# Last attention of a four-part block: head sums kept with heads on partitions, sorted by DMA, divided on GpSimd

## The chip, the cores and the metric

One core of one Trainium2 chip runs the whole program. The metric is the device time of one execution in microseconds (us); the median of the runs stands for the kernel.

## What is computed

The reference is a block of four residual parts on x of shape (4, 1024, 256): a cross attention, an expert layer, a second cross attention with 16 heads, and a last self attention with 16 heads of 16 channels over 4096 tokens in 4 batches. The change concerns the last part alone:

```
qkv = x @ W_qkv                        # x: layer norm of the block's x, 1024 tokens, 256 channels
logits = einsum('bqhd,bkhd->bhqk', q * scale, k)
x_pos = softmax over the registers and the tokens of the positive class, times v
x_neg = the same over the negative class
reg_out = (x_pos[:, :5] + x_neg[:, :5]) * 0.5      # 5 register tokens
tok_out = where(pos, x_pos, x_neg)                 # each token takes its own class
out = concatenate([reg_out, tok_out]) @ W_proj + b_proj
x = x + tanh(g_ffn[1]) * out
```

The softmax is computed as exp(score) with the row's maximum taken off first, then a product with v in which one more column gives the sum of the exponentials, and last a division by that sum.

## The kernel before

The last attention runs in 16 units (UNITS), one for each batch and group of four heads, u // 4 and u % 4. A unit has 16 steps: 2 halves of 512 queries times 8 blocks of 128 keys. In a step TensorE makes four score tiles, one for each head (scores2, L1530), in three PSUM banks used in turn; ScalarE turns each into exponentials (exps, L1012); TensorE multiplies them by the staged values (values2, L1521) and adds them up in bank 7 over the 8 key blocks of a half. In each half bank 7 ends with four heads on 32 partitions each: 16 rows of sums with v, one row of the sum of exponentials, 15 rows of zeros, since VST holds v in columns 0 to 15 and ones in column 16 only.

In the same steps the row maxima of the *next* unit are made: 32 tiles of 128 x 1024 (max_tile, L1502), each reduced by VectorE (reduce_tile, L2065). Two tiles belong to a step. PLAN lists what TensorE puts behind each step and VectorE takes in the same order: tiles, two "rows" turns, where maxima are transposed and written (max_rows L1507, L2069), and two "out" turns. The order of the steps is shifted by two (ORDER is 2, 3, ... 15, 0, 1), the last two being those of the next unit. The 16th unit has no tiles of a next one (PLAN_LAST).

The result of a half goes this way. ScalarE copies bank 7 to SBUF (copy_out2, L1017). In the "out" turn TensorE transposes it in four pieces of 128 x 128 (L1512), VectorE takes the reciprocal of the sums, now one column for each head (L2076), and multiplies (L2079) into On2, which holds tokens on partitions. After the last unit, VectorE averages the register tokens (L2117), and for each of 8 chunks of 512 tokens TensorE transposes On2 (L1625), ScalarE copies (L1042), TensorE projects (L1640), VectorE adds to x (L2124) and SyncE writes the chunk out (L676).

GpSimd has one job in this stage: stage_values (L796) copies the values of unit u + 2 into VST when unit u's products are done. TensorE waits for it (s_vst) at the last step of each unit. Its tensor operation with ALU.pow appears twice earlier: L706 raises 8 variances on each partition to the power -0.5 in each batch of each layer norm, and L774 does it with 2 numbers on each partition. SyncE issues all DMAs in program order (body_sp): the row of maxima, the stacks for the next unit but one, the second row, more stacks.

The lines that matter, of the waits in stage_values and of the power:

```
pool.tensor_tensor(rstd[:, v], rstd[:, v], mhalf[:, v], ALU.pow).then_inc(s_rs, 1)    # L706, 128 x 8
pool.tensor_tensor(qgn, qgn, mhalf[:, 0:2], ALU.pow).then_inc(s_qc, 1)                 # L774, 128 x 2
for u in range(UNITS - 2):
    pool.wait_ge(s_pv2, 2 + 16 * (u + 1))
    stage_values(u + 2, u % 2)
```

Of the kernel before, what the change touches and what calls it, by code (L numbers as in the profile page):

```python
# [20 lines left out]
H, D = 16, 16  # L21
# [17 lines left out]
def build_program(nc, ins, out):  # L39
    ctx = ExitStack()  # L40
    with ctx:
# [213 lines left out]
        s_gb = sem("gated_bias")  # L255
        s_xb = sem("bias_added")
# [28 lines left out]
        On2 = R1[:, :].rearrange("p (k u n) -> p k (u n)", u=UNITS, k=TB)  # L285
# [18 lines left out]
        regn = R5[0:REG, 3072:4096].rearrange("p (b c) -> p b c", b=B)  # L304
        PR = W[:, 0:4096].rearrange("p (u j n) -> p u j n", u=2, j=4)
        XNf = XN[:, :, :, :].rearrange("p u i c -> p (u i c)")
        Oe2 = XNf[:, 0:1024].rearrange("p (u n) -> p u n", u=2)
        mro = XNf[0:16, 1024:1152].bitcast(BF16).rearrange("p (u n) -> p u n", u=2)
# [19 lines left out]
        QR = sm2[:, 240:280].rearrange("p (j b r) -> p j b r", j=2, b=B)  # L328
        simc = sm2[:, 280:312]
# [16 lines left out]
        rc2 = sm2[:, 792:808].rearrange("p (q j) -> p q j", q=4)  # L346
        simr = sm2[:, 808:840]
        s_wq3 = sem("wqkv_loaded")
# [4 lines left out]
        s_gb2 = sem("gated_bias2")  # L353
        s_xb2 = sem("bias2_added")
# [9 lines left out]
        s_kf = sem("k_copied")  # L364
# [36 lines left out]
        s_oe2 = sem("out2_copied")  # L401
        s_vst = sem("values_staged")
        s_vpre = sem("value_stage_preset")
        s_rc2 = sem("out2_recip")
# [3 lines left out]
        OnT2 = W[:, 0:2048].rearrange("p (u j n) -> p u j n", u=2, j=2)  # L408
# [38 lines left out]
        PLAN[20].insert(0, ("out", 0))  # L447
        PLAN[30].insert(0, ("out", 1))
        PLAN_LAST = [[] for _ in range(32)] + [[("out", 1)]]
        PLAN_LAST[2].append(("rows", 1))  # L450
        PLAN_LAST[20].append(("out", 0))
# [4 lines left out]
        SMALL = [("rows", 1), ("rows", 0), ("out", 0), ("out", 1)]  # L456
        SMALL_LAST = [("rows", 1), ("out", 0), ("out", 1)]

        def small_turn(u, what, arg):
            return 4 * u + (SMALL_LAST if u + 1 == UNITS else SMALL).index((what, arg))  # L460

# [10 lines left out]
        USERS.append(("small", small_turn(UNITS - 1, "out", 1)))  # L472
# [16 lines left out]
        def _(sp):  # L489
# [171 lines left out]

            def body_sp(u, j, last=False, load=True):
                store_row(j, 1, s_bfree, small_turn(u, "rows", 1) + 1, u)
                if load:
                    load_max_stacks(u + 2, j)
                if not last:
                    store_row(1 - j, 0, s_bfree, small_turn(u, "rows", 0) + 1, u + 1)
                if load:
                    sp.wait_ge(s_sco, 64 * (u + 1))
                    load_stacks(u + 2, j)  # L670

            for u in range(UNITS):
                body_sp(u, u % 2, last=u + 1 == UNITS, load=u + 2 < UNITS)
            for c in range(NC):
                sp.wait_ge(s_x3, NC + c + 1)
                sp.dma_start(out[c // 2].rearrange("(i p) c -> p i c", p=P)[:, 4 * (c % 2):4 * (c % 2) + 4, :],  # L676
                             X[:, 4 * c:4 * c + 4, :]).then_inc(s_out, 16)
# [4 lines left out]
        def _(pool):  # L682
# [92 lines left out]
            pool.tensor_scalar(bp2[:, :], bp2[:, :], gates[:, 3:4], None, ALU.mult).then_inc(s_gb2, 1)  # L775
# [14 lines left out]
            pool.wait_ge(s_vpre, 2)  # L790
            for j in range(2):
                pool.memset(VST[j][:, :, :, D:D + 1], 1.0).then_inc(s_vpre, 1)
# [13 lines left out]
            pool.wait_ge(s_gb2, 1)  # L806
            pool.wait_ge(s_xn, 4 * NC)
            for b in range(B):
                xs = X[:, TB * b:TB * b + TB, :]
                pool.tensor_tensor(xs, xs, bp2[:, :].unsqueeze(1).to_broadcast([P, TB, C]), ALU.add).then_inc(s_xb2, 1)  # L810
# [6 lines left out]
        def _(act):  # L817
# [219 lines left out]
            for c in range(NC):  # L1037
                n = NC + c
                act.wait_ge(s_onT, n + 1)
                if c >= 2:  # L1040
                    act.wait_ge(s_wo, n - 1)
                act.copy(OnT2[:, c % 2], bank(2 * (c % 2), 2).rearrange("p (j t) -> p j t", j=2)).then_inc(s_onc, 1)  # L1042
# [3 lines left out]
        def _(pe):  # L1046
# [432 lines left out]
            def register_sum(b):  # L1479
                pe.wait_ge(s_rk, 2 * b + 2)  # L1480
                pe.matmul(bank(7)[0:REG, 0:C], Rsel, omk.rearrange("p j n -> p (j n)"),
                          start=True, stop=True).then_inc(s_rsm, 1)
# [25 lines left out]

            def out_turn(o, half, seen):
                pe.wait_ge(s_oe2, seen)  # L1510
                for i in range(4):
                    mm = pe.transpose(o[:, P * i:P * i + P], Oe2[:, half, P * i:P * i + P], identF[:, :])  # L1512
                mm.then_inc(s_turn, 1)
# [21 lines left out]
            def body_pe(u, j, loads, last=False):  # L1535
# [3 lines left out]
                def turns(entries):  # L1539
                    for what, arg in entries:  # L1540
                        if what == "tile":
                            max_tile(p + arg, arg, jn)
                        elif what == "rows":
# [3 lines left out]
                        else:  # L1547
                            out_turn(take_third("small", small_turn(u, what, arg)), arg, 2 * u + 2 + arg)
# [4 lines left out]
                for n, s in enumerate(ORDER):  # L1553
# [19 lines left out]
                    turns(plan[2 * n + 1])  # L1573
                if last:
                    values2(u, 15, j)
                    turns(plan[32])
# [39 lines left out]
            pe.wait_ge(s_avg, 1)  # L1616

            def transposes2(c):
                n = NC + c
                if c >= 2:  # L1620
                    pe.wait_ge(s_onc, n - 1)
                for j in range(2):
                    for i in range(4):
                        b, t = c // 2, 4 * (c % 2) + i
                        mm = pe.transpose(bank(2 * (c % 2) + j)[:, P * i:P * i + P],  # L1625
                                          On2[:, t, C * b + P * j:C * b + P * j + P], identF[:, :])
                mm.then_inc(s_onT, 1)

            transposes2(0)
            for c in range(NC):  # L1630
                n = NC + c
                if c + 1 < NC:
                    transposes2(c + 1)
                pe.wait_ge(s_onc, n + 1)
                if c >= 2:
                    pe.wait_ge(s_x3, n - 1)
                for i in range(4):
                    o = bank(4 + 2 * (c % 2) + i // 2)[:, C * (i % 2):C * (i % 2) + C]
                    for j in range(2):
                        mm = pe.matmul(o, OnT2[:, c % 2, j, P * i:P * i + P], wproj[:, j, :],  # L1640
                                       start=(i % 2 == 0 and j == 0), stop=(j == 1), skip_group_check=True)
                mm.then_inc(s_wo, 1)
# [532 lines left out]
```

## Time and profile before

| what | value |
|---|---|
| median of 3 runs | 1346.36 us (1345.57 to 1346.88) |
| the profiled execution's own time | 1345.22 us |
| its span | 1343.5 us |
| granted TensorE clock over the span | 0.958 of full |
| TensorE busy | 1224.0 us (91%) |
| VectorE busy | 1009.9 us (75%) |
| ScalarE busy | 831.2 us (62%) |
| GpSimd busy | 219.2 us (16%) |

The span is what the profile covers; the time of the same execution is 1.7 us longer. The busy share of an engine is a mean over stages with different limits. The last attention fills the second half of the span: its first results are copied at 647 us, its last unit ends near 1300 us, and the projection follows.

### The profile page before, as it was taken

Reading aid. Unit: us, or ns where it says so; the run is one execution under the profiler, and the core shown is the slowest. Engines: PE = TensorE matmul, PEld = TensorE weight load, DVE = VectorE, ACT = ScalarE, POOL = GpSimd, SP = SyncE. Lnnn points to the kernel's source line nnn. Section 1 sums busy time; section 2 is a strip of 40 time slices with the busy share of each in tenths; the row PEclk is TensorE's granted clock in tenths of the full one; section 3 lists DMA queues with packets and bytes.
Section 4 is the critical chain, followed back from the end, with each engine's and each line's share of the span. In section 5 each row is a group of like instructions: output and inputs, shape, how many; then the busy total and the mean of one; then the engine's idle time right before and its main releaser. Section 6 shows DMA issues by size and latency. Waiting matters only on the chain.

```text
span 1343.5 us, 26339 instructions
## 1 busy us (share of the span) xinstructions
PE 1224.0 (91%) x10562; PEld 570.5 (42%) x10562; DVE 1009.9 (75%) x1507; ACT 831.2 (62%) x1460; POOL 219.2 (16%) x167
## 2 busy tenths in 40 slices
PE   4988992999999899888999999999999999999988
PEld 3566682555558456244323233233233232332337
DVE  4896587565536749457999999999999999999702
ACT  2223293677762652113878778887888878887861
POOL 2130024455651332720000000000000000000000
PEclk9878895999999999798999999999999999999999
DMA  6100006676510234803334442443424433243003
GB/s 187 26 1 15 1 14 111 119 135 125 92 29 1 94 118 147 141 3 51 62 62 86 73 64 54 71 87 64 69 51 78 86 59 65 51 87 50 2 1 125
DMA packets 78826, 92.55 MB, mean 69 GB/s; under 512 B 15211, under 2 KB 53357, under 8 KB 78705
## 3 DMA queue, kind: packets, MB, share of 16 engines
q1 hardware_dynamic: 78704, 90.87, 34.0%
q8 instruction: 84, 1.38, 0.5%
q14 instruction: 38, 0.30, 0.1%
HBM read 67.02 MB, written 23.80 MB: 68 GB/s over the span
## 4 chain that ended last, share of the span: by engine, by line
PE 60%; DVE 29%; ACT 5%; issue 2%; DMA 1%; SPq 1%; POOL 1%; DVEq 0%; ACTq 0%; POOLq 0%
DVE sm L2065 19%; PE ps L1530 10%; PE ps L1521 9%; PE ps L1502 6%; PE ps L1391 3%; ACT W L1012 3%; PE ps L1297 2%; PE ps L1640 2%; PE ps L1288 2%; PE ps L1289 2%; PE ps L1215 2%; PE ps L1350 2%; PE ps L1457 2%; PE ps L1512 1%; PE ps L1255 1%
## 5 line engine op out<-in xcount | busy, mean ns | idle before, releaser
L2065 DVE TENSOR_REDUCE sm<-ps 128x1 f32<-128x1024 f32 x512 | 599.6, 1217 | 31.5 <-PE ps L1502 28.2
L1012 ACT ACTIVATE W<-ps 128x512 f32<-128x512 f32 x1024 | 534.8, 605 | 138.1 <-PE ps L1530 134.3
L1530 PE MATMUL ps<-R 99*32 99x512 bf16 x4096 | 318.5, 383 | 6.3 <-ACT W L1012 3.2
L1521 PE MATMUL ps<-W,R 128*32 128x512 f32 x2048 | 265.2, 594 | 0.7 <-ACT W L1012 0.7
L1530 PEld LDWEIGHTS ps<-R 99*32 99x32 bf16 x4096 | 86.1, 94 | 225.1 <-ACT W L1012 167.5
L796 POOL COPY R<-R 128x512 f32<-128x512 f32 x16 | 9.8, 613 | 633.1 <-PE ps L1521 633.1
L1502 PE MATMUL ps<-R 50*128 50x512 bf16 x512 | 90.5, 395 | 12.6 <-DVE sm L2065 9.8
L1502 PE MATMUL ps<-KM,R 50*128 50x512 bf16 x512 | 87.3, 384 | 9.6 <-DVE sm L2065 6.7
L936 ACT ACTIVATE R<-ps 77x512 f32<-77x512 f32 x128 | 75.0, 592 | 23.4 <-PE ps L1289 14.1
L1521 PEld LDWEIGHTS ps<-W,R 128*32 128x32 f32 x2048 | 63.0, 111 | 42.2 <-ACT W L1012 1.4
L1848 DVE TENSOR_REDUCE small<-ps 128x4 bf16<-128x308 f32 x128 | 57.5, 473 | 22.8 <-PE ps L1255 22.6
L739 POOL COPY R<-R 4x2048 bf16<-4x2048 bf16 x32 | 60.5, 1890 | 59.6 <-ACT R L918 53.7
L1502 PEld LDWEIGHTS ps<-R 50*128 50x128 bf16 x512 | 22.1, 93 | 91.4 <-issue 46.3
L1502 PEld LDWEIGHTS ps<-KM,R 50*128 50x128 bf16 x512 | 22.0, 93 | 89.7 <-issue 48.4
L1391 PE MATMUL ps<-R,W 128*128 128x512 f32 x128 | 57.9, 595 | 0.0
L1673 DVE TENSOR_SCALAR XN<-X,mv,rstd 128x256 f32<-128x256 f32 x128 | 46.6, 431 | 10.2 <-PE ps L1082 9.6
L1288 PE MATMUL ps<-R 100*77 100x512 bf16 x128 | 49.0, 383 | 0.0
L1289 PE MATMUL ps<-R 77*77 77x512 bf16 x128 | 48.6, 380 | 0.0
L1867 DVE RECIPROCAL small<-ps 128x16 f32<-128x16 f32 x32 | 8.2, 258 | 47.1 <-PE ps L1306 47.1
L1253 PE MATMUL ps<-R 77*128 77x308 bf16 x128 | 38.7, 302 | 4.1 <-DMA R<-x_parts 4.0
L704 POOL TENSOR_SCALAR rstd<-mv 128x8 f32<-128x8 f32 x16 | 9.0, 564 | 201.4 <-DVE mv L1655 176.4
L2076 DVE RECIPROCAL sm<-ps 128x16 f32<-128x16 f32 x32 | 8.2, 258 | 44.6 <-PE ps L1512 44.6
(260 smaller groups left out, 1613.0 us busy)
## 6 DMA issues: line engine op xcount, KB each, us to landing
R<-x_parts SPq DMA_DIRECT2D x96, 128.0 KB, 4.9
R<-q_parts SPq DMA_DIRECT2D x192, 64.0 KB
R<-q_parts SPq DMA_DIRECT2D x96, 128.0 KB
R<-k_parts SPq DMA_DIRECT2D x96, 128.0 KB
x_parts<-R SPq DMA_DIRECT2D x8, 768.0 KB, 7.0
q_parts<-R SPq DMA_DIRECT2D x24, 256.0 KB, 2.6
k_parts<-R SPq DMA_DIRECT2D x24, 256.0 KB, 2.6
X<-in_x SPq DMA_DIRECT2D x4, 1024.0 KB, 10.0
```

The source lines that it names most:

```text
L739: pool.tensor_copy(Xs[m // 2 % 3][SR:SR1, :, 512 * (m % 2):512 * (m % 2) + 512], mrow1[:, m % 2].unsqueeze(1).to_broadcast([4, 4, 512])).t ...
L936: act.activation(P1[:, m % 2, j, :], score_bank1(n)[0:KX, :], ACT.Exp, scale=0.25).then_inc(s_e1, 1)
L1012: act.activation(PR[:, s % 2, h, :], third_bank("score", 64 * u + n), ACT.Exp, scale=0.25).then_inc(s_sfree, 1)
L1288: pe.matmul(o, K1s[:, 4 * hg + j, KX * b:KX * b + KX], Xs[u % 3][:, j, t], start=True, stop=False)
L1289: pe.matmul(o, I4[:, 0:KX], mb1[:, t], start=False, stop=True).then_inc(s_sc, 1)
L1391: mm = pe.matmul(o[:, 512 * j:512 * j + 512], wqkv[:, i, C * kind + P * j:C * kind + P * j + P], XNT3[:, i, 512 * c:512 * c + 512], start= ...
L1502: mm = pe.matmul(pl[:, 512 * i:512 * i + 512], QMH[j][h][v, P * q:P * q + P], KM[j][v, h, :], start=True, stop=True)
L1521: mm = pe.matmul(bank(7)[32 * h:32 * h + 32, :], VST[j][:, k, h, :], PR[:, s % 2, h, :], start=(k == 0), stop=(k == TB - 1))
L1530: mm = pe.matmul(o[32 * c:32 * c + 32, :], KST[j][0:MAX_ROW + 1, h, t:t + 32], QST[j][0:MAX_ROW + 1, h, 512 * (s // 8):512 * (s // 8) + 51 ...
L1673: ins_ = dve.tensor_scalar(ln_chunk_buf(c)[:, i, :], X[:, 4 * c + i, :], mv[:, 4 * c + i, 0:1], rstd[:, 4 * c + i:4 * c + i + 1], ALU.subt ...
L1848: dve.tensor_reduce(Mn[:, u % 2, q, :], bank(n % 2)[:, 0:4 * KX].rearrange("p (j n) -> p j n", j=4), AX, ALU.max, negate=True).then_inc(s_ ...
L2065: dve.tensor_reduce(MX[:, half, h, q:q + 1], bank(2 * ((p + 1) % 2), 2), AX, ALU.max).then_inc(s_tfree, 1)
```

## The change

VST now holds ones in columns 16 to 31, so that bank 7 holds, for each head, 16 rows of sums with v and under them 16 equal rows with the sum of the exponentials. ScalarE copies it as before. SyncE then sorts each half with 8 DMAs from SBUF to SBUF: 4 put the 16 rows of v of each head into OT2, where head channels lie on partitions (16 heads by 16 channels in two halves j of 128) and tokens along them; 4 put the 16 rows of sums onto the same partitions of Den2. GpSimd raises Den2, 64 partitions by 512, to the power -1 and multiplies OT2 by it. OT2 is the stationary operand that the projection wants. The two "out" turns leave PLAN, the transposes and copies of the projection are gone, and 14 of its 32 tiles of 128 tokens are placed in the 14 steps of the last unit (project2). The registers are averaged in OT2's layout. Three of the eight chunks are written out before the sort of the last half. On GpSimd stage_values comes between the two divisions of a unit.

Cut to its core (semaphores renamed, register_sum and register_kept put into the new layout, and declarations are left out):

```diff
@@ SyncE
+            def sort_out(u, half):
+                b, rows, j = u // 4, 64 * (u % 2), u // 2 % 2
+                sp.wait_ge(s_oe2, 2 * u + half + 2)
+                if u >= 2:
+                    sp.wait_ge(s_nd2, 2 * (2 * (u - 2) + half + 1))
+                for h in range(4):
+                    v = slice(rows + 16 * h, rows + 16 * h + 16)
+                    sp.dma_start(OT2[v, j, b, 512 * half:512 * half + 512],
+                                 Oe2[32 * h:32 * h + 16, half, :]).then_inc(s_od2[half], 16)
+                    sp.dma_start(Den2[half][v, :], Oe2[32 * h + 16:32 * h + 32, half, :]).then_inc(s_od2[half], 16)
             def body_sp(u, j, last=False, load=True):
                 store_row(j, 1, s_bfree, small_turn(u, "rows", 1) + 1, u)
                 if load:
                     load_max_stacks(u + 2, j)
+                sort_out(u, 0)
                 if not last:
                     store_row(1 - j, 0, s_bfree, small_turn(u, "rows", 0) + 1, u + 1)
+                else:
+                    for c in range(3):
+                        store_out(c)
                 if load:
                     sp.wait_ge(s_sco, 64 * (u + 1))
                     load_stacks(u + 2, j)
+                sort_out(u, 1)
@@ GpSimd
+            pool.memset(mone, -1.0).then_inc(s_vpre, 1)
             for j in range(2):
-                pool.memset(VST[j], 0.0).then_inc(s_vpre, 1)
+                pool.memset(VST[j], 1.0).then_inc(s_vpre, 1)
-            for u in range(UNITS - 2):
-                pool.wait_ge(s_pv2, 2 + 16 * (u + 1))
-                stage_values(u + 2, u % 2)
+            def divide_out(u, half):
+                b, rows, j = u // 4, 64 * (u % 2), u // 2 % 2
+                v, n = slice(rows, rows + 64), 2 * u + half
+                pool.wait_ge(s_od2[half], 128 * (u + 1))
+                den = Den2[half][v, :]
+                o = OT2[v, j, b, 512 * half:512 * half + 512]
+                pool.tensor_tensor(den, den, mone[v, :].to_broadcast([64, 512]), ALU.pow).then_inc(s_nd2, 1)
+                pool.wait_ge(s_nd2, 2 * n + 1)
+                pool.tensor_tensor(o, o, den, ALU.mult).then_inc(s_nd2, 1)
+                pool.wait_ge(s_nd2, 2 * n + 2)
+
+            for u in range(UNITS):
+                divide_out(u, 0)
+                if u + 2 < UNITS:
+                    pool.wait_ge(s_pv2, 2 + 16 * (u + 1))
+                    stage_values(u + 2, u % 2)
+                    pool.wait_ge(s_vst, u + 3)
+                divide_out(u, 1)
@@ ScalarE
             def copy_out2(u, half):
                 act.wait_ge(s_pv2, 16 * u + 8 * half + 10)
+                if u >= 1:
+                    act.wait_ge(s_od2[half], 128 * u)
                 act.copy(Oe2[:, half, :], bank(7)).then_inc(s_oe2, 1)
-            for c in range(NC):
-                act.copy(OnT2[:, c % 2], ...)
@@ TensorE
-            def out_turn(o, half, seen): ...
+                    if last:
+                        project2(n)
+            def project2(i):
+                c, q = i // 4, i % 4
+                n = NC + c
+                if i == 0:
+                    pe.wait_ge(s_tfree, PAIRS0 + 32 * (UNITS - 1))
+                    pe.wait_ge(s_avg, 2)
+                if i == 4 * (NC - 2):
+                    pe.wait_ge(s_avg, 4)
+                if q == 0 and c >= 2:
+                    pe.wait_ge(s_x3, n - 1)
+                o = bank(2 * (c % 2) + q // 2)[:, C * (q % 2):C * (q % 2) + C]
+                for j in range(2):
+                    mm = pe.matmul(o, OT2[:, j, c // 2, 512 * (c % 2) + P * q:512 * (c % 2) + P * q + P],
+                                   wproj[:, j, :], ...)
+                if q == 3:
+                    mm.then_inc(s_wo, 1)
-            def transposes2(c): ...
+            for i in range(14, NT):
+                project2(i)
@@ VectorE
-            def normalise2(n, o, u, half): ...
             for u in range(UNITS):
+                if u + 1 == UNITS:
+                    dve.wait_ge(s_nd2, 16 * (B - 1))
+                    average_registers(slice(0, B - 1))
                 body_dve(u, last=u + 1 == UNITS)
+            for c in range(3):
+                x4_chunk(c)
+            dve.wait_ge(s_nd2, 4 * UNITS)
+            average_registers(slice(B - 1, B))
+            for c in range(3, NC):
+                x4_chunk(c)
```

## Rows read from the trace of the kernel before

**Rows 1.** The chain of waits, by line, in the stretch 655 to 1230 us.

```profile
by line: DVE sm L2065 38.4%; PE ps L1530 18.5%; PE ps L1521 16.2%; PE ps L1502 11.7%; ACT W L1012 5.1%; PE ps L1512 2.9%; DVE R L2079 2.1%; issue 1.8%; DVE sm L2076 1.3%; ACT XN L1017 1.2%; PE ps L1507 1.0%; DVEq L2060 0.1%; ACTq L1011 0.0%
```

**Rows 2.** Busy us of each engine in one stretch, then TensorE clock, DMA share, GB/s.

```profile
core 0: us, PE busy (x) PEld busy (x) DVE busy (x) ACT busy (x) POOL busy (x), PEclk, DMA share, GB/s
862.00:903.00 41.00, 39.60 (x443) 12.30 (x444) 37.75 (x38) 32.60 (x64) 0.61 (x1) 1.00 0.38 71
```

**Rows 3.** Timeline of GpSimd, 579 to 1343 us: start, duration, line; idle before it.

```profile
668.00 0.61 POOL L796 COPY R<-R 128x512 f32<-128x512 f32 x1 [88.72 <-PE ps L1521]
710.48 0.61 POOL L796 COPY R<-R 128x512 f32<-128x512 f32 x1 [41.88 <-PE ps L1521]
...
1220.31 0.61 POOL L796 COPY R<-R 128x512 f32<-128x512 f32 x1 [41.86 <-PE ps L1521]
```

**Rows 4.** The out turn: ns min/median/max by line, and VectorE's maximum tile.

```profile
L1512 PE MATMUL ps<-identF,XN x128: 272/273/330, 657.1 to 1301.1; 128*128 128x128 f32 x128
...
L2076 DVE RECIPROCAL sm<-ps x32: 256/258/258, 657.8 to 1301.5; 128x16 f32<-128x16 f32 x32
...
L2079 DVE TENSOR_TENSOR R<-ps,sm x32: 424/424/426, 658.1 to 1301.8; 128x256 f32<-128x256 f32 x32
...
L2065 DVE TENSOR_REDUCE sm<-ps x512: 1202/1215/1226, 556.1 to 1268.1; 128x1 f32<-128x1024 f32 x171
```

**Rows 5.** GpSimd's powers and their neighbour L704: ns min/median/max by line.

```profile
L706 POOL TENSOR_TENSOR rstd<-rstd,mhalf x16: 1665/1807/2605, 10.0 to 452.8; 128x8 f32<-128x8 f32 x16
...
L774 POOL TENSOR_TENSOR sm<-sm,mhalf x1: 725/725/725, 397.5 to 397.5; 128x2 f32<-128x2 f32 x1
...
L704 POOL TENSOR_SCALAR rstd<-mv x16: 238/306/2571, 9.7 to 452.4; 128x8 f32<-128x8 f32 x16
```

**Rows 6.** GpSimd's adds and copies: ns min/median/max by line.

```profile
L810 POOL TENSOR_TENSOR X<-X,bp x4: 4497/4498/4505, 561.4 to 574.8; 128x2048 f32<-128x2048 f32 x4
...
L796 POOL COPY R<-R x16: 609/614/615, 553.0 to 1220.3; 128x512 f32<-128x512 f32 x16
```

**Rows 7.** Timeline of SyncE's DMA issues and of ScalarE's first copy, 640 to 662 us.

```profile
643.64 3.04 SPq L600 DMA_DIRECT2D R<-k_parts  x6
...
648.25 0.26 SPq L609 DMA_DIRECT2D R<-class_rows  x1
655.11 0.32 SPq L650 DMA_DIRECT2D max_rows<-XN  x1
...
646.91 0.61 ACT L1017 COPY XN<-ps 128x512 f32<-128x512 f32 x1
```

**Rows 8.** Issue of the short row's DMA: ns, and us from issue to landing.

```profile
L650 SPq DMA_DIRECT2D max_rows<-XN x32: 308/318/327, 602.6 to 1271.3; - x32
...
DMA to landing us min/median/max: 1.3/1.6/3.1
```

**Rows 9.** The chain of waits at the last unit's end, in order of time.

```profile
1294.93 0.86 PE ps L1521 x8
1297.11 0.86 PE ps L1521 x8
1298.89 1.11 PE ps L1521 x8
...
1331.94 6.92 PE ps L1640 x32
1338.89 1.28 DVE X L2124
```

**Rows 10.** Output DMA, L676: issue ns, and us from issue to landing.

```profile
L676 SPq DMA_DIRECT2D out<-X x8: 372/372/405, 1310.8 to 1340.2; - x8
...
DMA to landing us min/median/max: 2.9/2.9/3.0
```

More of the change, by code:

```diff
@@ L401, in build_program @@
         s_oe2 = sem("out2_copied")
+        s_od2 = [sem(f"out2_sorted{n}") for n in range(2)]
+        s_nd2 = sem("out2_divided")
         s_vst = sem("values_staged")
         s_vpre = sem("value_stage_preset")
-        s_rc2 = sem("out2_recip")
+        s_rc2 = sem("register_recip")
         s_avg = sem("registers_averaged")
         s_out = sem("output_written")
-        OnT2 = W[:, 0:2048].rearrange("p (u j n) -> p u j n", u=2, j=2)
         CLS_DONE = 23
@@ L446, in build_program @@
         PLAN[18].insert(0, ("rows", 0))
-        PLAN[20].insert(0, ("out", 0))
-        PLAN[30].insert(0, ("out", 1))
-        PLAN_LAST = [[] for _ in range(32)] + [[("out", 1)]]
+        PLAN_LAST = [[] for _ in range(32)]
         PLAN_LAST[2].append(("rows", 1))
-        PLAN_LAST[20].append(("out", 0))
         PAIRS0 = 33
         TURNS = sum(len(x) for x in PLAN)
-        SMALL = [("rows", 1), ("rows", 0), ("out", 0), ("out", 1)]
-        SMALL_LAST = [("rows", 1), ("out", 0), ("out", 1)]
+        SMALL = [("rows", 1), ("rows", 0)]
         def small_turn(u, what, arg):
-            return 4 * u + (SMALL_LAST if u + 1 == UNITS else SMALL).index((what, arg))
+            return 2 * u + SMALL.index((what, arg))
         USERS = [("score", n) for n in range(4 * SHIFT)]
@@ L787, in _ @@
                 pool.wait_ge(s_kw2[n], 48 * (NC // 2))
+            pool.memset(mone, -1.0).then_inc(s_vpre, 1)
             for j in range(2):
-                pool.memset(VST[j], 0.0).then_inc(s_vpre, 1)
-            pool.wait_ge(s_vpre, 2)
-            for j in range(2):
-                pool.memset(VST[j][:, :, :, D:D + 1], 1.0).then_inc(s_vpre, 1)
+                pool.memset(VST[j], 1.0).then_inc(s_vpre, 1)
+            pool.wait_ge(s_vpre, 3)
             pool.wait_ge(s_vf, NC)
@@ L1036, in _ @@
                 body_act(u, last=u + 1 == UNITS)
[L1037 to L1042, printed above, removed]
         @block.tensor
@@ L1507, in max_rows @@
                 pe.transpose(o[0:16, 0:P], MX[:, half].rearrange("p j q -> p (j q)"), identF[:, :]).then_inc(s_turn, 1)
[L1509 to L1513, printed above, removed]
             def values2(u, s, j):
@@ L1542, in turns @@
                             max_tile(p + arg, arg, jn)
-                        elif what == "rows":
+                        else:
                             o = take_third("small", small_turn(u, what, arg))
@@ L1573, in body_pe @@
                     turns(plan[2 * n + 1])
+                    if last:
+                        project2(n)
                 if last:
                     values2(u, 15, j)
-                    turns(plan[32])
+            def project2(i):
[9 more added lines that the diff above has]
+                o = bank(2 * (c % 2) + q // 2)[:, C * (q % 2):C * (q % 2) + C]
+                for j in range(2):
+                    mm = pe.matmul(o, OT2[:, j, c // 2, 512 * (c % 2) + P * q:512 * (c % 2) + P * q + P],
+                                   wproj[:, j, :], start=(q % 2 == 0 and j == 0), stop=(j == 1),
+                                   skip_group_check=True)
+                if q == 3:
+                    mm.then_inc(s_wo, 1)
             pe.sem_inc(s_pv2, 2)
@@ L1613, in _ @@
                 body_pe(u, u % 2, (u + 1) // 2 + 1, last=u + 1 == UNITS)
[L1616 to L1642, printed above, removed]
+            for i in range(14, NT):
+                project2(i)
         @block.vector
@@ L2105, in body_dve, with average_registers, x4_chunk @@
                     else:
[L2106 to L2111 removed]
+                        rows_turn(n, third_bank("small", small_turn(u, what, arg)), arg, s_bfree)
+                    n += 1
+            def average_registers(batches):
+                for j in range(2):
+                    o = OT2[:, j, batches, 0:REG]
+                    dve.scalar_tensor_tensor(o, o, 0.5, regT[:, j, batches, :], ALU.mult, ALU.add).then_inc(s_avg, 1)
+            def x4_chunk(c):
+                dve.wait_ge(s_wo, NC + c + 1)
+                dve.wait_ge(s_xb, B + c // 2 + 1)
+                xs = X[:, 4 * c:4 * c + 4, :]
+                dve.scalar_tensor_tensor(xs, bank(2 * (c % 2), 2).rearrange("p (i n) -> p i n", i=4),
+                                         gates[:, 3:4], xs, ALU.mult, ALU.add).then_inc(s_x3, 1)
             for u in range(UNITS):
+                if u + 1 == UNITS:
+                    dve.wait_ge(s_nd2, 16 * (B - 1))
+                    average_registers(slice(0, B - 1))
                 body_dve(u, last=u + 1 == UNITS)
[L2116 to L2125 removed]
+            for c in range(3):
+                x4_chunk(c)
+            dve.wait_ge(s_nd2, 4 * UNITS)
+            average_registers(slice(B - 1, B))
+            for c in range(3, NC):
+                x4_chunk(c)
 def kernel(**inputs):
```

65 lines of the change are left out of this document (19 added, 46 removed).

## Prediction

> **What bounds the kernel now.** I read the chain of waits for the middle of the last attention first, then the busy times of one unit, then GpSimd's own timeline. The chain goes round through VectorE's maxima (38%), TensorE's scores, values and maximum tiles (46% together) and a little ScalarE [rows 1]. The reader is to see a loop of three engines that are all nearly full: in 41 us TensorE is busy 39.6, VectorE 37.75, ScalarE 32.6 [rows 2]. GpSimd is busy 0.61 us in that stretch. Its copies come at 668.00, 710.48 and so on to 1220.31, 14 of them, so a unit takes (1220.31 - 668.00) / 13 = 42.49 us, and GpSimd is idle for 41.9 of it [rows 3]. That idle time is what the change means to use: 41.9 us for two divisions. Everything hangs on whether they fit.
>
> **What it removes inside the units.** For each half, four transposes, a reciprocal of 0.258 us and a multiplication of 0.424 us on VectorE [rows 4]. That is 2 x 0.68 = 1.36 us of VectorE for each unit, and the transposes on TensorE lie in the same loop; in the chain the three lines have 6.3% [rows 1], which of 42.49 us is 2.7 us. Part of that comes back as other waits of the loop, so between 0.6 and 1.4 us for each of 15 units, if nothing else bound it; I take 1.1, in all 16 us.
>
> **What it removes at the end.** Now the last product of values starts at 1298.89 and ends near 1299.8, and the span ends at 1343.5: a tail of 43.7 us [rows 9]. In the last unit a step takes 2.18 us [rows 9]. A projection tile of 128 tokens is a quarter of a chunk, and two chunks took 6.92 us, so 0.87 us [rows 9]. A step without tiles uses TensorE for about 0.86 us of values and as much for scores, 1.74; with a projection tile it is 2.6, which is 0.43 us over 2.18, and over 14 steps 6 us. Behind the last product then come a copy (0.7), eight sorting DMAs, the division, the average (0.3), 8 tiles that need it (6.9), the last addition (1.3) and the output's issue and landing (3.3) [rows 7, 9, 10]. The other ten tiles lie beside the sort and the division. A short issue takes 0.32 us and its landing 1.6 [rows 8], so the sort is 8 x 0.32 plus 1.6 to 3, near 5 us. The new tail is 6 + 0.7 + 5 + 0.3 + 6.9 + 1.3 + 3.3 = 23.5 us plus one division T, against 43.7: a gain of 20 - T.
>
> **What it adds to SyncE and ScalarE.** SyncE gets 16 DMAs in a unit, at 0.32 us [rows 8] 5 us, ahead of the row of maxima for the next unit's first half and ahead of the other row. At 0.5 us, as the longer loads need (six in 3.04, rows 7), it is 8 us. TensorE wants the first row at step 14 and VectorE makes it at step 9, about 13 us earlier, so I cost it at nothing; if that cover goes, it is at most 4 us a unit. The copy waits for a sort one unit old: nothing.
>
> **What it adds to GpSimd.** A division is a power and a multiplication on 64 partitions by 512. The multiplication goes by the addition of 2048 elements with two inputs in 4.498 us [rows 6]: 512 / 2048 of it is 1.12 us. The copy of 512 in 0.61 us [rows 6] is its lower end, and neither end matters here.
>
> The power is another thing. With 8 elements on each partition it took 1.665 us at the least and 1.807 in the middle, while a scalar addition of the same 128 x 8 just before took 0.238 at the least; with 2 elements it took 0.725 [rows 5]. So 6 more elements cost 0.94 us, 157 ns for each, and about 0.41 us does not depend on the size. An addition costs 4.498 / 2048, or 2.2 ns for each: the power is some 70 times dearer. By that line 512 elements take 0.41 + 512 x 0.157 = 80.7 us. Fewer partitions should not help: all partitions of the rows go side by side, and what counts is how many elements lie along each. The upper ends: the medians give (1.807 - 0.725) / 6 = 180 ns and 92.7 us; the whole of 1.665 laid on 8 elements is 208 ns and 106.6 us. The lower end: an operation as cheap as an addition, 1.1 us. Between ends so far apart I take 80.7, since it comes from the same operation on the same engine, and from its two shortest executions, and the stretch concerned has little else that touches SBUF.
>
> The Trainium skill speaks for the other end. The page GPSIMD Engine Reference, section "Elementwise — side-by-side cycle accounting", counts about 2.6 cycles an element for an operation with two tensors and gives 4497 ns for an addition of 2048, whatever the share of partitions. The trace agrees for additions (4498 ns, rows 6) but not for the power. By that rule the division would be some 2.2 us and the sum that of the first rival.
>
> **The sum.** T = 80.7 + 1.12 + 0.1 for two waits = 81.9 us. Two of them and a copy are 164.4 us a unit, against 42.49: GpSimd becomes the bound. TensorE waits for s_vst at the last step of unit u + 1, and that copy is queued behind divide_out(u, 0); SyncE's sorts wait for the division two units back. In that pause the other engines stand still; while GpSimd divides, they need only 42 us to hand over the next two halves. So GpSimd never starves, and its queue is a plain sum:
> - the first copy ends at 647.5, SyncE is busy with stacks until 648.5 [rows 7], and the sort takes 5 to 7 us: start at 655;
> - 32 divisions x 81.9 = 2621;
> - 14 copies x 0.61 = 8.5;
> - the tail after the last division: 0.3 + 6.9 + 1.3 + 3.3 = 12. TensorE has been idle by then, and at half the clock the 8 tiles would take 7 us more.
>
> The span is 655 + 2621 + 8.5 + 12 = 3296.5 us. The profiled execution's time is 1.7 us over its span, and the median 1.1 over that: 3299, so I say 3300. The gains of 16 and 20 us vanish in it, since the other engines are idle three quarters of the time. The other ends give 655 + 32 x 93.9 + 20.5 = 3680 and 655 + 32 x 107.8 + 20.5 = 4125.
>
> **Rival 1, faster: the power is nearly as cheap as an addition.** Its first elements might pay for something that 512 don't pay again. With T = 2.3 us both divisions fit into 41.9, the gains stand: 1346.4 - 16 - 17.7 = 1312. This is the case that the page's rule gives. For it: only 2 and 8 elements are seen, and nothing longer. Against it: those two already show a slope of 157 ns, and all sixteen with 8 elements took over 1.66 us. It decides at T = 20.9: 655 + 32 T + 20.5 is then 1346. The power would have to cost under 39 ns an element, a quarter of the slope. 0.17.
>
> **Rival 2: the long loop runs better, but GpSimd still bounds.** If the slope falls to between 40 and 120 ns, the time is 1350 to 2700. 0.08.
>
> **Rival 3: cheap power, and the change gains nothing.** A loop of three full engines can give the 16 us back, and a T of 15 to 20 takes the tail's gain: within 0.2% of before. 0.02.
>
> **Forecast:** GpSimd's power binds at the rate of the rows, 3150 to 4000 us: 0.73. It has its own range, from the shortest rows' slope to nearly the full 208 ns.
>
> **How the numbers follow.** 0.2% of 1346 is 2.7 us, about what a measurement can tell from no change. Faster is rival 1 with the low end of rival 2's neighbourhood: 0.18. Same 0.02. Slower is the forecast and rival 2: 0.80. To leave out no more than 2 in 10 the range takes in the forecast's and nearly all of rival 2's, and leaves rival 1 and 3: 1700 to 4000.
>
> **What the profile after would show.** GpSimd busy over 75% of the span, with 32 powers of 64 x 512 at 80 us or more and 32 multiplications near 1.1 us; the chain made of that line; TensorE under 45%, waiting at the last step of each unit for L796's successor; the copies of values 164 us apart in place of 42.5. If the powers take 1 to 3 us, the argument is wrong at the slope, and then the copies should be about 41.4 us apart and the tail after the last values near 26 us. If the powers are dear but the time is above 655 + 32 T + 20, GpSimd did starve, and the overlap is wrong.

## The result and the profile after

The changed kernel takes 3355.29 us (median) against 1346.62 us of the kernel before in the same comparison: the ratio is 2.489, 95% interval 2.4855 to 2.4925. The prediction was 3300 us. The profiled execution took 3356.33 us, with a span of 3354.5 us. The median is that of four runs, three of 3352.49 to 3356.33 us and one of 4371.99, which the ratio and the profile leave out and whose cause stays open.

Part 1 of the changed kernel's page, and the first two lines of part 4, the chain that ended last:

```profile
PE 1237.6 (37%) x10378; PEld 560.5 (17%) x10378; DVE 990.8 (30%) x1446; ACT 825.7 (25%) x1452; POOL 2879.4 (86%) x230
...
POOL 80%; PE 13%; DVE 4%; SPq 1%; issue 1%; DMA 1%; ACT 1%; POOLq 0%; DVEq 0%
POOL W L830 39%; POOL XN L830 39%; PE ps L1415 1%; POOL R L832 1%; PE ps L1321 1%; PE ps L1312 1%; PE ps L1313 1%; PE ps L1239 1%; PE ps L1374 1%; PE ps L1481 1%; DVE sm L2077 1%; PE ps L1279 1%; PE ps L1277 1%; PE ps L1330 1%; PE ps L1423 1%
```

VectorE and ScalarE do nearly the same work as before, in a span two and a half times as long. GpSimd went from 219 us to 2879 us, and one line, L830, is 78% of the chain. L830 is the power. Below are its instructions (ns min/median/max) on the two tiles that hold Den2, W for the first halves and XN for the second, 16 each, and the multiplication L832 by W:

```profile
L830 POOL TENSOR_TENSOR W<-W,sm x16: 81908/81913/81947, 659.8 to 3169.1; 64x512 f32<-64x512 f32 x16
L830 POOL TENSOR_TENSOR XN<-XN,sm x16: 81908/81912/81915, 743.8 to 3252.4; 64x512 f32<-64x512 f32 x16
...
L832 POOL TENSOR_TENSOR R<-R,W x16: 1253/1257/1260, 741.8 to 3251.0; 64x512 f32<-64x512 f32 x16
```

GpSimd's timeline, which answers to [rows 3]: the copies of values are now 910.45 - 743.13 = 167.3 us apart, and between them GpSimd does not rest.

```profile
659.78 81.95 POOL L830 TENSOR_TENSOR W<-W,sm 64x512 f32<-64x512 f32 x1 [75.96 <-DMA W<-XN]
741.81 1.25 POOL L832 TENSOR_TENSOR R<-R,W 64x512 f32<-64x512 f32 x1
743.13 0.61 POOL L809 COPY R<-R 128x512 f32<-128x512 f32 x1
743.82 81.91 POOL L830 TENSOR_TENSOR XN<-XN,sm 64x512 f32<-64x512 f32 x1
825.80 1.25 POOL L832 TENSOR_TENSOR R<-R,XN 64x512 f32<-64x512 f32 x1
827.14 81.92 POOL L830 TENSOR_TENSOR W<-W,sm 64x512 f32<-64x512 f32 x1
909.13 1.26 POOL L832 TENSOR_TENSOR R<-R,W 64x512 f32<-64x512 f32 x1
910.45 0.61 POOL L809 COPY R<-R 128x512 f32<-128x512 f32 x1
```

The busy times of one such period, where [rows 2] show a stretch of one unit before:

```profile
744.00:911.00 167.00, 41.59 (x450) 12.10 (x442) 38.16 (x34) 34.22 (x66) 166.70 (x5) 0.62 0.11 21
```

TensorE, VectorE and ScalarE are busy for 41.6, 38.2 and 34.2 us of the 167, about what one unit took before, and stand still for the rest. TensorE's granted clock is 0.62 in this stretch, where it was 1.00. Who waited for whom, 660 to 3330 us (us in total, times, longest):

```profile
ACT W L1040 <- PE ps L1549: 1781.4, 236, 126.4
DVE sm L2077 <- PE ps L1527: 1707.3, 100, 127.1
PEld ps L1540 <- POOL R L809: 1653.8, 14, 125.5
```

TensorE waited 14 times for the copy of values, up to 125.5 us each, and the other two waited for TensorE. The copy itself takes 0.61 us; it was late because two powers stand ahead of it in GpSimd's queue.

### The profile page after: what moved, and what is told of

Its sections match the earlier page's. It is cut to its first block, busy times and chain, and to the rows that moved or that the text cites. A ratio compares the mean times of both kernels' runs of the same rounds, so it can differ in the third digit from the quotient of the medians.

```text
span 3354.5 us, 26252 instructions
## 1 busy us (share of the span) xinstructions
PE 1237.6 (37%) x10378; PEld 560.5 (17%) x10378; DVE 990.8 (30%) x1446; ACT 825.7 (25%) x1452; POOL 2879.4 (86%) x230
## 4 chain that ended last, share of the span: by engine, by line
POOL 80%; PE 13%; DVE 4%; SPq 1%; issue 1%; DMA 1%; ACT 1%; POOLq 0%; DVEq 0%
POOL W L830 39%; POOL XN L830 39%; PE ps L1415 1%; POOL R L832 1%; PE ps L1321 1%; PE ps L1312 1%; PE ps L1313 1%; PE ps L1239 1%; PE ps L1374 1%; PE ps L1481 1%; DVE sm L2077 1%; PE ps L1279 1%; PE ps L1277 1%; PE ps L1330 1%; PE ps L1423 1%
## 5 line engine op out<-in xcount | busy, mean ns | idle before, releaser
L830 POOL TENSOR_TENSOR W<-W,sm 64x512 f32<-64x512 f32 x16 | 1310.6, 81913 | 77.1 <-DMA W<-XN 76.0
L830 POOL TENSOR_TENSOR XN<-XN,sm 64x512 f32<-64x512 f32 x16 | 1310.6, 81912 | 1.3
L1540 PE MATMUL ps<-W,R 128*32 128x512 f32 x2048 | 284.1, 632 | 1649.6 <-POOL R L809 1649.6
L1549 PE MATMUL ps<-R 99*32 99x512 bf16 x4096 | 325.5, 393 | 0.6 <-DVE sm L2068 0.5
L1608 PE MATMUL ps<-wproj,R 128*128 128x256 f32 x128 | 33.9, 411 | 366.5 <-DVE X L2119 366.5
L2113 DVE SCALAR_TENSOR_TENSOR R<-R,sm 128x15 f32<-128x15 f32 (+1 forms) x4 | 0.5, 168 | 375.9 <-POOL R L832 375.8
L1608 PEld LDWEIGHTS ps<-wproj,R 128*128 128x128 f32 x128 | 24.5, 202 | 378.5 <-DVE X L2119 368.0
L798 POOL TENSOR_TENSOR R<-R 128x1024 bf16<-128x1024 f32 x8 | 17.0, 2124 | 42.2 <-ACT R L1016 42.2
L793 POOL TENSOR_TENSOR R<-R 128x1024 bf16<-128x1024 f32 x8 | 17.1, 2135 | 38.5 <-ACT R L1005 38.5
```

The lines of the kernel that those rows point to most:

```text
L830: pool.tensor_tensor(den, den, mone[v, :].to_broadcast([64, 512]), ALU.pow).then_inc(s_nd2, 1)
L1540: mm = pe.matmul(bank(7)[32 * h:32 * h + 32, :], VST[j][:, k, h, :], PR[:, s % 2, h, :], start=(k == 0), stop=(k == TB - 1))
L1549: mm = pe.matmul(o[32 * c:32 * c + 32, :], KST[j][0:MAX_ROW + 1, h, t:t + 32], QST[j][0:MAX_ROW + 1, h, 512 * (s // 8):512 * (s // 8) + 51 ...
L1608: mm = pe.matmul(o, OT2[:, j, c // 2, 512 * (c % 2) + P * q:512 * (c % 2) + P * q + P], wproj[:, j, :], start=(q % 2 == 0 and j == 0), sto ...
```

## The experiments

The cuts of code leave out most semaphore increments, and "..." marks lines that are left out.

**Half as many elements.** In divide_out:

```diff
-                pool.tensor_tensor(den, den, mone[v, :].to_broadcast([64, 512]), ALU.pow)
+                pool.tensor_tensor(den[:, 0:256], den[:, 0:256], mone[v, :].to_broadcast([64, 256]), ALU.pow)
```

> The power takes 256 of the 512 sums of each half; the others are multiplied in as they are, so half of the results are not divided. Theory (a price for each element along a partition, about 159 ns, and 0.4 us besides): the power takes 0.4 + 256 x 0.159 = 41.1 us, a division 42.5, and the time is 660 + 32 x 42.6 + 10 + 16 = 2050 us. Rival (a price for the instruction or for the partitions in use, not for the elements): the power stays near 82 us and the time near 3355 us.

It took 2047.91 us (one run). GpSimd's groups, 660 to 2040 us:

```profile
L830 POOL TENSOR_TENSOR W<-W,sm 64x256 f32<-64x256 f32 x16 | 657.9, 41116 | 77.2 <-DMA W<-XN 76.0
L830 POOL TENSOR_TENSOR XN<-XN,sm 64x256 f32<-64x256 f32 x16 | 657.8, 41114 | 1.3
```

The power took 41.1 us and the time followed: 32 times 40.8 us less is 1306 us, and 3355 - 2048 is 1307. So the price goes by the elements along a partition, and the time by the price.

**A table of powers.** The kernel before, with one power of another shape after some of the copies of values, on a scratch tile:

```diff
                 stage_values(u + 2, u % 2)
+                if u in TAB:
+                    r, m = TAB[u]
+                    pool.memset(pt, 37.0)
+                    pool.tensor_tensor(pt[0:r, 0:m], pt[0:r, 0:m], pe1[0:r, 0:m], ALU.pow)
```

> The kernel before, with powers of eight shapes put into GpSimd's idle time on a scratch tile, so the output is unchanged: 128x16, 128x32, 64x64, 128x64, 64x128, 128x128, 128x192, 128x512. Theory (linear in the elements of a partition, whatever the number of partitions): 3.0, 5.5, 10.6, 10.6, 20.8, 20.8, 31 and 82 us, the same for 64 and 128 partitions, and the time stays at 1346.6 us, since all lie in idle time. Rival (the time goes by all elements, so 64 partitions are twice as cheap): the 64-partition shapes take half of the 128-partition ones, and 128x512 takes 164 us and lengthens the end. Rival (GpSimd's reads take SBUF from VectorE): the maxima tiles beside the powers last over 1.22 us each and the time rises by several us.

It took 1348.69 us, where the runs of the kernel before on the same chip gave 1346.57 to 1352.83. From its timeline of GpSimd (start, duration):

```profile
672.60 10.57 POOL L826 TENSOR_TENSOR W<-W,XN 128x64 f32<-128x64 f32 x1
...
715.08 10.54 POOL L826 TENSOR_TENSOR W<-W,XN 64x64 f32<-64x64 f32 x1
...
757.57 20.79 POOL L826 TENSOR_TENSOR W<-W,XN 128x128 f32<-128x128 f32 x1
...
800.07 20.77 POOL L826 TENSOR_TENSOR W<-W,XN 64x128 f32<-64x128 f32 x1
...
842.56 31.01 POOL L826 TENSOR_TENSOR W<-W,XN 128x192 f32<-128x192 f32 x1
...
885.05 5.43 POOL L826 TENSOR_TENSOR W<-W,XN 128x32 f32<-128x32 f32 x1
...
927.54 2.90 POOL L826 TENSOR_TENSOR W<-W,XN 128x16 f32<-128x16 f32 x1
...
1224.92 82.17 POOL L826 TENSOR_TENSOR W<-W,XN 128x512 f32<-128x512 f32 x1
```

The line is straight: (82.17 - 2.90) / 496 = 0.160 us for each element along a partition, and 0.34 us besides. Half the partitions cost the same. Here every number raised was 37, in the changed kernel they were the real sums, and 512 of them took 82.17 and 81.91 us, so the values made no difference that matters. And 82 us of power in an idle engine cost the kernel nothing that can be measured; VectorE's maxima beside it kept their mean of 1218 ns (1225 to 1307 us), as in the kernel before. What hurts is what is queued behind it.

**The change without its price.** The power on 16 of the 512 sums, all else of the change kept (so 31 of 32 results are not divided):

```diff
-                pool.tensor_tensor(den, den, mone[v, :].to_broadcast([64, 512]), ALU.pow)
+                pool.tensor_tensor(den[:, 0:16], den[:, 0:16], mone[v, :].to_broadcast([64, 16]), ALU.pow)
```

> The power takes only 16 of the 512 sums of each half, so 31 of 32 results are multiplied by the sum and not divided. All else of the change stands. Theory (the power alone costs the 2010 us; the rest of the change gains 16 us in the units and some 16 at the end): a power of 0.4 + 16 x 0.159 = 3.0 us, units 41.4 us apart, the time near 1315 us. Rival (three full engines give the gain back, or the 16 more DMAs of a unit hold up the rows): units stay at 42.5 us or more and the time is 1330 to 1350 us.

It took 1317.07 us, ratio 0.9751 (0.9726 to 0.9775). ScalarE's copies of results follow each other, in this run and in the kernel before, like this (both timelines of ScalarE; two copies belong to a unit):

```profile
668.16 0.61 ACT L1017 COPY XN<-ps 128x512 f32<-128x512 f32 x1
689.40 0.61 ACT L1017 COPY XN<-ps 128x512 f32<-128x512 f32 x1
```

```profile
672.06 0.60 ACT L1047 COPY XN<-ps 128x512 f32<-128x512 f32 x1
692.36 0.60 ACT L1047 COPY XN<-ps 128x512 f32<-128x512 f32 x1
```

Half a unit went from 21.24 to 20.30 us, so a unit from 42.49 to 40.6: 28 us over 15 units. The end, from the timeline of the run with a power of 16:

```profile
1286.17 0.59 ACT L1047 COPY XN<-ps 128x512 f32<-128x512 f32 x1 [1.46 <-PE ps L1540]
...
1296.22 1.26 POOL L832 TENSOR_TENSOR R<-R,XN 64x512 f32<-64x512 f32 x1
1297.52 0.24 DVE L2113 SCALAR_TENSOR_TENSOR R<-R,sm 128x5 f32<-128x5 f32 x2 [16.89 <-POOL R L832]
1297.67 2.47 DVE L2119 SCALAR_TENSOR_TENSOR X<-ps,gates,X 128x1024 f32<-128x1024 f32 x2
...
1299.01 13.39 PE L1608 MATMUL ps<-wproj,R 128*128 128x256 f32 x48 [7.53 <-DVE X L2119]
```

From the last copy to the end of the span it is 1317.1 - 1286.2 = 30.9 us, against 1343.5 - 1300.0 = 43.5 before. TensorE stands 7.5 us in it, for an addition (L2119) that VectorE does only after the averages (L2113), for which it waits on the last division. Behind that wait TensorE's granted clock was 0.80 (1299 to 1313 us), and its 12 tiles took 13.39 us, or 1.12 each.

**The order at the end.** The same, power of 16 and all, with the average bound to the first half of the last unit, where all register tokens lie:

```diff
-            dve.wait_ge(s_nd2, 4 * UNITS)
+            dve.wait_ge(s_nd2, 4 * UNITS - 2)
             average_registers(slice(B - 1, B))
...
                 if i == 4 * (NC - 2):
                     pe.wait_ge(s_avg, 4)
+                if i == 4 * (NC - 1):
+                    pe.wait_ge(s_nd2, 4 * UNITS)
```

> The run with a power of 16 sums (31 of 32 results not divided), with one thing more: the registers are averaged and chunk 3 is added once the first half of the last unit is divided, and only the last chunk's tiles wait for the second half. Theory (TensorE's 7.5 us at the end came from VectorE, which stood at the last division ahead of chunk 3's addition, and not from the division as such): that wait goes and the time falls from 1317 to about 1309 us. Rival (another wait takes its place, as the last half is divided no sooner): TensorE waits some 7 us at the last chunk instead, and the time stays at 1315 to 1317 us.

It took 1305.97 us, ratio 0.9682 (0.9657 to 0.9706), 11 us below the run with a power of 16; the two medians come from different comparisons. Within one execution, the last copy came at 1284.51 and the span ended at 1304.8: 20.3 us in place of 30.9. The wait went and no other took its place. That is 10.6 us for a wait of 7.5: the other 3 are the tiles, of which 18 now run without a gap in 15.81 us, or 0.88 each.

**The reciprocal on VectorE.** Full computation; VectorE makes the reciprocal of the same 64 x 512 tile, behind the maximum tiles 16 and 30 of each unit, and GpSimd multiplies (in the last unit the additions and averages are put in an order that suits; left out here):

```diff
+            def recip_out(u, half):
+                v = slice(64 * (u % 2), 64 * (u % 2) + 64)
+                dve.wait_ge(s_od2[half], 128 * (u + 1))
+                dve.reciprocal(Den2[half][v, :], Den2[half][v, :]).then_inc(s_rc2, 1)
...
-                pool.tensor_tensor(den, den, mone[v, :].to_broadcast([64, 512]), ALU.pow)
+                pool.wait_ge(s_rc2, B + n + 1)
```

> The changed kernel with the power replaced by VectorE's reciprocal of the same 64x512 tile, GpSimd keeping the multiplication; full computation. Theory (only the power was dear): a reciprocal near 0.6 us, twice a unit on VectorE, in place of 1.36 us there; units near 41.8 us apart, the tail near 26 us in place of 43.7, the time 1318 to 1325 us. Rival (the loop of three engines or the added DMAs take the gain): 1335 us or more. Rival (VectorE's reciprocal of 512 from SBUF is several times dearer than an element a cycle): units over 43 us and the time above 1346 us.

It took 1471.75 us, ratio 1.09 (1.0875 to 1.0925): the second rival of the expectation, above 1346 us. Its instructions (ns min/median/max), and VectorE's timeline round one of them:

```profile
L2117 DVE RECIPROCAL W<-W x16: 3344/3347/3351, 673.4 to 1426.3; 64x512 f32<-64x512 f32 x16
```

```profile
774.58 1.22 DVE L2076 TENSOR_REDUCE sm<-ps 128x1 f32<-128x1024 f32 x1 [0.33 <-PE ps L1526]
775.83 3.34 DVE L2117 RECIPROCAL W<-W 64x512 f32<-64x512 f32 x1
779.10 3.41 DVE L2076 TENSOR_REDUCE sm<-ps 128x1 f32<-128x1024 f32 x3
784.81 0.28 DVE L2080 TENSOR_SCALAR XN<-ps 16x128 bf16<-16x128 f32 x1 [2.30 <-PE ps L1531]
```

3.34 us for 512 elements (in SBUF) against 0.258 for 16 (from PSUM) [rows 4] is 6.2 ns for each. The expectation's 0.6 us could have been seen to be wrong beforehand: the kernel before has one reciprocal of this length in an earlier stage, on 128 partitions (groups of VectorE, by form):

```profile
L1971 DVE RECIPROCAL W<-W 128x512 f32<-128x512 f32 x1 | 3.4, 3353 | 1.6 <-ACT W L991 1.6
```

It took 3.35 us, and half the partitions cost VectorE the same. The units are (1343.62 - 678.21) / 13 = 51.2 us apart by the copies of values. Two reciprocals are 6.7 us of that; against units of 40.6 us it is 10.6, so each costs more than itself. The trace shows why. TensorE waits for the maxima behind each reciprocal, 3.13 us at 757.95 and 3.40 us at 780.31, and then runs at the lower of its two clocks, 1.2 of 2.4 GHz: granted 0.50 from 780.0 to 784.8 us, where eight products of values took 1.93 us in place of 1.03. From one copy of values to the next (729.20 to 780.66) TensorE is busy 44.4 us at a granted clock of 0.90; with the power of 16 it was 40.0 us of a unit, at 1.00. The two waits and these 4.4 us are the 10.6, within half a microsecond. Other places for the reciprocals in VectorE's order were not tried.

**Packed sums.** Both engines charge by the elements along a partition, and the sort had laid the 2048 different sums of a half out as 64 rows of 512, 16 equal ones for each head. So the sums go to 128 partitions by 16 before the power, and back afterwards; the last unit keeps the direct sort and VectorE's reciprocal, and the end has the better order of the run above. In SyncE's sort_out, and a second function with the way back:

```diff
+                    sp.dma_start(DN[0, half], Oe2[16:128:32, half, :])
...
+                    sp.wait_ge(s_clw2, ...)
+                    sp.dma_start(Pk2[half], DN[0, half].rearrange("h (i n) -> (h i) n", n=16))
...
+            def spread_out(u, half):
+                sp.wait_ge(s_rc2, B + k + 1)
+                sp.dma_start(DN[1, half].rearrange("h (i n) -> (h i) n", n=16), Pk2[half])
+                sp.wait_ge(s_clw, ...)
+                for h in range(4):
+                    sp.dma_start(Den2[half][rows + 16 * h:rows + 16 * h + 16, :],
+                                 DN[1, half, h:h + 1].to_broadcast([16, 512]))
...
+                    pool.tensor_tensor(Pk2[half], Pk2[half], mone[:, :].to_broadcast([P, 16]), ALU.pow)
```

> Full computation. The sums of a half (4 rows of 512) go through DRAM onto 128 partitions by 16 before the power and through DRAM back onto the 64 partitions, 16 times each; the last unit keeps the direct sort and takes VectorE's reciprocal; its registers are averaged as soon as the first half is divided, and only the last chunk's four tiles wait for the second. Theory (the power costs 0.16 us for each element along a partition, so 128x16 costs 2.9 us, and what is left of the change is worth what the run with a power of 16 showed): units 40.7 us apart as there, TensorE's wait of 7.5 us at the end gone, the time 1306 to 1312 us against 1317 of that run. Rival (SyncE's new waits on its own writes and on the power hold up the row of maxima or the stacks): TensorE waits at the row's or the stacks' DMA, units over 41.5 us, the time over 1325 us.

It took 1396.56 us, ratio 1.0337 (1.0319 to 1.0355). The power was 2.90 us as expected, and the units were 47.9 us apart by the copies of values, (1291.38 - 669.27) / 13: the rival held. SyncE was the trouble. What its queue waited for, 700 to 1300 us, and the head of that stretch's chain by line:

```profile
SPq L681 <- POOL XN L851: 65.9, 23, 5.2
SPq L676 <- DMA den_rows<-XN: 60.5, 13, 5.8
SPq L684 <- DMA den_rows<-XN: 36.0, 25, 3.0
```

```profile
by line: DVE sm L2104 30.9%; PE ps L1574 22.5%; PE ps L1565 19.3%; PE ps L1552 14.3%; issue 12.3%; PE ps L1557 0.8%
```

SyncE waits 162 us for the sums in 600 us. TensorE's stalls carry no name here ("issue", 12.3%, against 1.8% in [rows 1]). SyncE's and TensorE's timelines round one of them:

```profile
803.94 1.72 SPq L684 DMA_DIRECT2D W<-den_rows  x4
805.71 0.42 SPq L647 DMA_DIRECT2D max_rows<-XN  x1
807.43 0.63 SPq L649 DMA_DIRECT2D R<-max_rows  x1
```

```profile
803.60 0.61 PE L1552 MATMUL ps<-R 50*128 50x512 bf16 x4
809.55 1.47 PE L1574 MATMUL ps<-R 99*32 99x512 bf16 x12 [5.34 <-issue]
```

The row of maxima goes out behind the sums, its load is issued at 807.43, and the next unit's first scores, which need it, start 2.1 us later. TensorE has then stood for 5.3 us, and its granted clock is 0.50 from 809.5 to 812 us; over 700 to 1300 us it is 0.92. The profile does not name the releaser, so that it is the row is read from the order and the times.

**The same on GpSimd's queue.** The seven DMAs of a half that carry the sums, and their waits, move from SyncE to GpSimd, and ScalarE's copy now waits for the power of the unit before:

```diff
-                    sp.dma_start(DN[0, half], Oe2[16:128:32, half, :])
+                    pool.wait_ge(s_oe2, n + 2)
+                    pool.dma_start(DN[0, half], Oe2[16:128:32, half, :])
...
-                    sp.dma_start(Den2[half][rows + 16 * h:rows + 16 * h + 16, :], ...)
+                        pool.dma_start(Den2[half][rows + 16 * h:rows + 16 * h + 16, :], ...)
```

> As the run with the packed sums, full computation, but the seven DMAs of each half that carry the sums through DRAM are issued and waited for by GpSimd on its own queue; SyncE keeps the four that sort the values, and none of its waits on the sums. Theory (what cost the packed kernel its gain was SyncE: 46 us of issues and waits in a unit, with the row of maxima behind them): units near 40.7 us apart, as with the power of 16, and the tail of 20.5 us that the packed run had, so 1305 to 1312 us. Rival (GpSimd's own DMAs are too slow: seven issues and four round trips for a half exceed the 20 us it has): GpSimd's chain takes over 40 us a unit and units follow it, over 1330 us. Rival (the descriptors that GpSimd writes take SBUF or DMA time from the others): maxima tiles over 1.22 us or TensorE waits at stacks, 1315 to 1340 us.

It took 1306.32 us, ratio 0.968 (0.9651 to 0.9709), with the full computation: 3.2% below the kernel before. GpSimd's timeline of one half:

```profile
738.85 0.62 POOL L835 DMA_DIRECT2D den_rows<-XN  x1 [0.29 <-POOL R L852]
740.85 0.57 POOL L837 DMA_DIRECT2D XN<-den_rows  x1 [1.39 <-DMA den_rows<-XN]
743.03 2.93 POOL L839 TENSOR_TENSOR XN<-XN,sm 128x16 f32<-128x16 f32 x1 [1.61 <-DMA XN<-den_rows]
746.25 0.61 POOL L841 DMA_DIRECT2D den_rows<-XN  x1 [0.30 <-POOL XN L839]
748.27 1.95 POOL L844 DMA_DIRECT2D W<-den_rows  x4 [1.41 <-DMA den_rows<-XN]
753.43 1.27 POOL L852 TENSOR_TENSOR R<-R,W 64x512 f32<-64x512 f32 x1 [3.21 <-DMA W<-den_rows]
```

This half takes 15.9 us from first to last, most of it waits; the other half of a unit, with the stacks' loads under way, took 25.3 (713.23 to 738.55). The copies of values are 41.78 us apart, 1.2 more than a unit, so GpSimd falls behind by some 15 us over the 13 units between them, and the copy's slack of nearly a unit takes it. ScalarE's copies run at 20.29 us, as with the power of 16. So SyncE's order, and not the DMAs as such, had taken the gain of the packed kernel. The first rival was near: GpSimd's chain is longer than a unit, so with enough more units it would bind again.

**The projection behind the last unit.** The last kernel with all 32 tiles after the last unit (the last averages, additions and stores are put in the order that suits; left out here):

```diff
-                    if last:
-                        project2(n)
...
-            for i in range(14, NT):
+            for i in range(NT):
                 project2(i)
```

> The run with the packed sums on GpSimd's queue (full computation), with all 32 projection tiles behind the last unit. Theory (a projection tile lengthened the last unit's steps from 2.18 to 2.90 us, so of 14 x 0.87 = 12.2 us only 2.1 were hidden): the last unit 10.1 us shorter, the tail 12.2 us longer, the time 1306.3 + 2 = 1308.4 us. Rival (what the prediction took, 0.43 us a step, so that 6.2 us are hidden): 1312.5 us.

It took 1307.45 us, ratio 0.9695 (0.9673 to 0.9718), which the interval does not tell from the kernel with the early tiles (0.968); the rival's 1312.5 lies outside it. In the profiles the last three half-unit copies are 1234.99, 1253.18 and 1270.71 here and 1239.85, 1263.91 and 1286.29 there, so two halves take 35.7 us against 46.4: the 14 tiles lengthened the last unit by 10.7 us. The stretch from the last copy to the end is 1303.1 - 1270.7 = 32.4 us here and 1306.6 - 1286.3 = 20.3 there: 12.1. By these two profiles the early start is worth the difference, 1.4 us.

## Why the prediction was right

**The bound.** The step that decided, a line through powers of 2 and 8 elements extended to 512, held: 81.9 us measured, 80.7 forecast. The table shows that the line is straight and that partitions don't count. It also shows that the choice of the shortest executions was right: by its line 8 elements cost 0.34 + 8 x 0.160 = 1.62 us, where the shortest took 1.665 and the median 1.807; the line through the medians would have given 92.7. The page GPSIMD Engine Reference of the Trainium skill, section "Elementwise — side-by-side cycle accounting", counts about 2.6 cycles an element for an operation with two inputs. That holds in size for the multiplication (1.26 us for 512 elements, 1.12 from the addition's rate in [rows 6]), but not for the power, which costs 160 ns an element against 2.2. The prediction has the page say this for any share of the partitions; the page has no sentence on that, and for the power it is the table that shows it.

**The sum.** The span came out at 3354.5, 58 us over 3296.5, and the terms account for it:

| term | forecast | measured | difference |
|---|---|---|---|
| first power starts | 655 | 659.8 | +4.8 |
| 32 divisions and 14 copies | 2629.5 | 3335.6 - 659.8 = 2675.8 | +46.3 |
| tail | 12 | 3354.5 - 3335.6 = 18.9 | +6.9 |

In the middle term a division is 1.4 us longer than 81.9: 1.2 by the power, 0.14 by the multiplication. The start is later for the most part because this execution came to the last attention later: ScalarE's first copy is at 650.80 us and not 646.91, and SyncE's loads of the stacks end 3.9 us later. That differs from one execution to the next (647.39 with 256 elements, 651.77 with 16). Only 0.9 us are the sort's, which took 7.4 us from its first issue to the first power, and not 6.5: its issues took 0.59 us each and not 0.32, which had been read from another DMA. The tail is longer for a reason that the prediction missed: it counted 8 tiles behind the last division, and there were 12, since VectorE adds chunk 3 only after the averages and TensorE's tiles from 20 on wait for that bank. These 12 took 12.7 us, or 1.06 each against 0.87; after its long wait TensorE's granted clock was 0.63 from 3337 to 3343 us, and 1.00 from there to 3350. The addition of chunk 3 ahead of them, 1.3 us, had not been counted either.

**The overlap.** GpSimd never starved, as forecast: between the first power and the last multiplication it is idle for 6 us in all, the pauses between one instruction and the next; the run with 256 elements shows the same (1.3 us before 16 powers, and 1.2 before the other 16 once the first start is taken off). The prediction's own sign for a starving GpSimd would have misled here. With a division of 83.4 us, pauses included, 655 + 32 T + 20.5 is 3343 us, and the span is 11 us above it; but these 11 us are the start (4.8) and the tail (6.9), as the table tells, and no wait.

**What the prediction got wrong without harm.** The gain in the units was put at 1.1 us each and is 1.9, above the 1.4 that it allowed for: after the out turns went, nothing else came up. The 14 early tiles were put at 6 us and cost 10.7, since a step went to 2.90 us and not to 2.6. What comes behind the last unit was put at 23.5 - 6 = 17.5 us plus a division, so 21.7 with one of 4.2, and was 30.9, for the missed order at the end. With a division of 4.2 us the forecast's terms give 16 + 20 - 4.2 = 32 us; the ratio of 0.9751 is 34 us of 1346.6. That these are so near is luck: 12 us more from the units stand against 5 and 9 us lost on the early tiles and the end. A slip of 0.2 us had no effect: the last product ends at 1300.0 [rows 9], not 1299.8. The rival that put the time at 1312 was right about what the change gives with a cheap power (1317 measured), and its condition, the cheap power, did not hold.

## What to carry to other kernels

Before an operation is moved to an idle engine, find that very operation on that engine, at two sizes if it can be had, and extend the line; the rate of additions says nothing of a power, nor that of a maximum anything of a reciprocal. Then look at what is queued behind it: 82 us in an idle queue cost nothing, and twice the same 82 us ahead of each copy of 0.6 us cost 125 us a unit. And where an operation is charged by elements along a partition, lay the distinct values across partitions first; here 16 equal copies of each sum had been raised to a power, and 128 x 16 instead of 64 x 512 turned 82 us into 2.9. With the DMAs for it in GpSimd's queue, and the better order at the end, the ratio went from 2.49 to 0.968; in SyncE's, ahead of the row of maxima, it was 1.034.

## What was not expected

VectorE's reciprocal costs 6.2 ns for each element along a partition (3.34 us for 512), where its maximum over 1024 takes 1.22 us, or 1.2 ns for each. In the run with that reciprocal TensorE's waits of 3.1 and 3.4 us cost more than their length, since it ran at a granted clock of 0.50 behind them. And seven DMAs a half, issued by GpSimd itself with four waits on them, did not slow the others: VectorE's maxima kept a mean of 1220 ns, as with the power of 16, and the half units 20.29 us.
